# Attention with a per-head bias: ScalarE instead of SyncE issues the loads of the next head group's bias

## The reference

```python
x = x + tanh(g_xattn[0]) * L0_xattn(layernorm(x), ctx, ctx, mask, relative_bias, ...)
# inside, with B, S, H, DH = 4, 512, 16, 16; relative_bias is (1, H, S, S) in float32
scores = einsum('bhqd,bhkd->bhqk', q, k) / sqrt(DH) + relative_bias
attn = softmax(where(mask, scores, -inf), axis=-1)
out = einsum('bhqk,bhkd->bhqd', attn, v)
```

## Time and profile before

| What | Value |
|---|---|
| Time, median of 3 runs | 987.95 us (987.23 to 991.28) |
| The profiled execution's own time | 987.71 us |
| Its span | 986.0 us |
| PE busy | 926.7 us, 94% |
| ACT, POOL, DVE busy | 508.7, 547.7, 581.9 us |
| Attention of the first layer, tiles of L624 | from 63.7 us to about 283 us |

### The profile page before, as it was taken

The page is one execution under the profiler, slowest core; times in us unless marked ns, Lnnn a source line. Parts: engine busy times, 40 slices in busy tenths (PEclk is TensorE's granted clock), DMA queues, the critical chain, the costliest instruction groups (busy, mean ns, idle before and its releaser), DMA issues. The chain is left out here.

```text
span 986.0 us, 22226 instructions
## 1 busy us (share of the span) xinstructions
PE 926.7 (94%) x8245; PEld 541.8 (55%) x8246; DVE 581.9 (59%) x1688; ACT 508.7 (52%) x708; POOL 547.7 (56%) x586
## 2 busy tenths in 40 slices
PE   6989989899989999998999999988899999999998
PEld 2545545454447544454454455456365667777765
DVE  3857878687845634468888888837452222222226
ACT  2428878687863423326888988863301022222221
POOL 4338878688956921127988888851136312222223
PEclk9978999899998999998999999999999999999999
DMA  8572634527104423333242232311922212112217
GB/s 290 195 232 66 205 80 137 151 65 227 46 7 140 150 75 107 96 110 101 66 119 67 86 101 65 89 38 53 331 58 88 75 51 60 64 59 64 64 48 240
DMA packets 99985, 107.63 MB, mean 109 GB/s; under 512 B 18762, under 2 KB 83794, under 8 KB 99890
## 3 DMA queue, kind: packets, MB, share of 16 engines
q1 hardware_dynamic: 89026, 87.79, 29.4%
q10 hardware_dynamic: 7456, 9.18, 2.9%
q0 software_dynamic: 3408, 9.38, 2.7%
HBM read 76.92 MB, written 29.38 MB: 108 GB/s over the span
## 5 line engine op out<-in xcount | busy, mean ns | idle before, releaser
L682 ACT ACTIVATE pT<-ps 128x1024 f32<-128x1024 f32 x256 | 248.3, 1024 | 69.6 <-PE ps L558 69.5
L721 POOL TENSOR_TENSOR s<-nmax,s 128x512 f32<-128x512 f32 x188 | 189.1, 1041 | 37.1 <-DVE nmax L624 37.1
L624 DVE CUSTOM_DVE_ANT_0 xT<-ps,bias 128x512 f32<-128x512 f32 x256 | 166.6, 688 | 44.1 <-PE ps L541 33.5
L721 POOL TENSOR_TENSOR xT<-nmax,xT 128x512 f32<-128x512 f32 x160 | 163.7, 1040 | 38.5 <-DVE nmax L624 38.0
L624 DVE CUSTOM_DVE_ANT_0 s<-ps,bias 128x512 f32<-128x512 f32 x256 | 166.2, 688 | 32.0 <-PE ps L541 21.2
L541 PE MATMUL ps<-ks,qs 48*128 48x512 bf16 (+1 forms) x1024 | 169.3, 393 | 11.7 <-DVE nmax L624 6.6
L573 PE MATMUL ps<-pT,vq 128*32 128x512 f32 x1024 | 135.7, 606 | 5.7 <-ACT pT L682 5.4
L1622 POOL DMA_INDIRECT slots_out<-y,id x39 | 37.7, 968 | 130.6 <-DVE y L1952 123.9
L541 PEld LDWEIGHTS ps<-ks,qs 48*128 48x128 bf16 (+1 forms) x1024 | 39.9, 97 | 126.0 <-DVE nmax L624 93.9
L1706 PE MATMUL ps<-gu,xgT 128*128 x312 | 98.8, 460 | 0.7 <-ACT xgT L1790 0.7
L558 PEld LDWEIGHTS ps<-ident,xT 64*128 64x128 f32 x2048 | 75.0, 139 | 15.5 <-issue 4.6
(11 more groups left out here) (204 smaller groups left out, 1236.8 us busy)
## 6 DMA issues: line engine op xcount, KB each, us to landing
bias<-in_bias SPq DMA_DIRECT2D x14, 1024.0 KB, 7.4
qk_scratch<-parts SPq DMA_DIRECT2D x60, 128.0 KB
qs<-qk_scratch SPq DMA_DIRECT2D x64, 96.0 KB, 2.5
ks<-qk_scratch SPq DMA_DIRECT2D x64, 96.0 KB, 2.4
gu<-in_gate_up SPq DMA_DIRECT2D x8, 704.0 KB, 9.1
slots_in<-zeros SPq DMA_DIRECT2D x4, 1280.0 KB, 6.5
xg<-slots_in SPq DMA_DIRECT2D x39, 130.0 KB
qk_scratch<-parts ACTq DMA_DIRECT2D x36, 128.0 KB
```

Source lines behind the costliest of these rows:

```text
L624: nc.vector.tensor_tensor_reduce(at.s[n % 4][:, k, :], sb.ps[:, ring_bank(tile_place[u]), :], at.bias[:, j if per_head_bias else 0, k, :], ...
L682: nc.scalar.activation(at.pT[:, slot(m // HG, m % HG), 2 * half:2 * half + 2, :], sb.ps[:, 2 + 2 * half:4 + 2 * half, :], ACT.Exp).then_in ...
L721: nc.gpsimd.tensor_tensor(s, at.nmax[:, n % 4, k:k + 1].to_broadcast([P, S]), s, ALU.subtract).then_inc(pool_less_max, 1)
```

## The change

In each of the first three groups, the four bias loads of the next group leave SP's program. ACT issues them instead, in the steps of the last batch (`b == B - 1`): the load of slice `j` stands after the previous step's subtraction (and in step 15 after `keep_out`) and ahead of the exponentials of its own step. It waits for the same semaphore value as before. There are 12 such DMAs in all, of the same size, from the same source to the same place.

```diff
--- before.py
+++ after.py
@@ -516,10 +516,6 @@
                 if not last:
                     sp.wait_ge(scores_done, (hg * 4 + 4) * 16 + 16)
                     load_qk(sp, at, dram, per_head_bias, hg + 1, 0)
-                    for j in range(HG if per_head_bias else 0):
-
-                        sp.wait_ge(biased, at_order[hg * M + M - HG + j, QT - 1] + 1 + 2)
-                        load_bias(sp, at, bias_dram, hg + 1, j)
             groups(sp, body)
 
         @block.tensor
@@ -700,6 +696,9 @@
                         keep_out(*before(hg, b))
                     if first and m == 0:
                         subtract_max(1)
+                    if per_head_bias and b == B - 1 and not last:
+                        act.wait_ge(biased, at_order[hg * M + m, QT - 1] + 1 + 2)
+                        load_bias(act, at, bias_dram, hg + 1, j)
                     exps(hg, m, 0, exp0)
                     exps(hg, m, 1, exp1)
                     if not (last and m + 2 >= M):
```

## The result

The changed kernel is slower: the ratio of its time to the kernel before is **1.0104, 95% interval 1.0068 to 1.0140**, the medians are 996.93 and 987.95 us in nine executions each. Forecast were 1008 us and a range from 998 to 1020. The sign is right. The rise is about 10 us in place of 20.

A forecast was written before the change was run, and what follows sets the result against it. PE, busy 94% of the span, was taken as the bound, with 12.2 us lost at three boundaries. Each would lose 9.3 plus 1.5 us, 32.2 in all: +20.0 on 987.71, hence 1008 us, range 998 to 1020.

The forecast's parts named there:

- The boundaries, and only they: All time lost or gained lies at the three group boundaries, which would lose 32.2 us in place of 12.2.
- j = 0 at nothing: First bias load at a boundary: issued about 1 us later than by SP, landing about when needed, no cost.
- j = 1 issued before 113: Sign in the trace at the first boundary that would prove the forecast wrong; it expected issue at about 115.5.
- j = 1 behind step 12, issued at 115.5 and landing after 7.0 us: First boundary: load issued about 5 us later than now, lands at 122.5, stalling PE more than 4 us at tile 65.
- The chain through `keep_out` to j = 3: First boundary: PE's stall delays keep_out; j = 3 leaves at 127.0, lands at 132.4, and turn_out comes 9.3 us late.
- 1.5 us of lower clock behind the second stall: At each boundary, PE's slower clock after the wait at tile 73 adds 1.5 us, making 10.8.
- SP ... starts the next `load_qk` some 2 us earlier; ... that gives nothing: SP, rid of four issues at a boundary, starts this load sooner; needed only a batch later, it counts as nothing.
- even with 8 us: j = 2, issued near 118.5, lands by 126.5, covered by the wait for j = 3; uncovered, up to 1 us.
- the disputed price: Landing time of j = 1 on ACT's queue beside load_qk: between 5.3 and 10.5 us, taken as 7.0.
- the first rival: Loads on ACT's queue slow beside load_qk, j = 1 taking 10.5 us: 3.5 us more per boundary, 1018 us; chance 0.15.
- The moment of issue as the whole cause: At the boundaries, time from issue to landing stays on the path; the change moves only when loads are issued.
- The rival from the Trainium skill: Issuing from ACT only saves SP's issue time at the boundaries, so slightly faster: fourth rival, 985 us, chance 0.03.

The follow-up runs named there:

- e6_no_loads: The kernel before without the bias loads of groups 1 to 3 and DVE's waits for them; ratio 0.9889.
- e1: The change, but ACT issues j = 0 and 1 together ahead of step 12's exponentials, j = 2 and 3 together ahead of step 14's; ratio 1.0061.
- e7: e1 with SP also holding the next load_qk until DVE is done with the old group's last tile; ratio to the kernel before 1.0076.
- e10: The kernel before with j = 2 and 3 moved to ACT as a pair ahead of step 14's exponentials, SP keeping j = 0 and 1; ratio 1.0095.
- e12_change_no_qk: The change without the load_qk of batch 1 in groups 1 to 3; ratio to the kernel before 1.0057.
- e9: The kernel before with j = 0 and 1 moved to ACT as a pair ahead of step 12's exponentials, SP keeping j = 2 and 3; ratio 0.9987.
- e5_split: The kernel before, SP issuing, with each bias load cut into four 256 KB tiles, each with its own issue, semaphore and DVE wait; ratio 0.9890.
- e11_split_act: The change with each bias load cut into four tiles with a semaphore each, all issued by ACT at the change's places; ratio to the kernel before 1.0089.
- e4_no_ahead: The change, with ACT also waiting for the previous step's second exponential ahead of each bias load; ratio to the kernel before 1.0093.
- e3_j3_early: The change, but j = 3 issued together with j = 2 ahead of step 14's exponentials; ratio to the kernel before 1.0079.
- e2: The change, but j = 1 issued together with j = 0 ahead of step 12's exponentials; ratio to the kernel before 1.0084.

## Why the prediction was half right

- **The boundaries, and only they.** Right: the 9.5 us of added loss there go with the 10.3 of the ratio, and e6_no_loads gives 11 us where the earlier trace rows had 12.2.
- **j = 0 at nothing.** Right. I had it leave about 1 us later than from SP; it left 1 us earlier, since ACT runs ahead. The sign "j = 1 issued before 113" came true on the clock (110.81), but this execution stands 3.3 us ahead; on the scale of the kernel before it is 114.1.
- **j = 1 behind step 12, issued at 115.5 and landing after 7.0 us.** Right as a mechanism, both terms too large. Counted from the matmuls of tiles 64 and 65 (112.40 here, 115.71 before), it left 1.6 us ahead of them in place of 0.2, and landed in 5.6 us. I had named 0.6 us as the most that ACT could run ahead; it was 1.4. Together 2.8 us at the first boundary.
- **The chain through `keep_out` to j = 3.** Right in the trace of the change: `keep_out` idles 3.18 us for PE, and j = 3 goes out with it. I had it leave at the end of `keep_out`, it leaves at the start (0.6 us). With j = 1 too early to stall PE for long, the chain is the shorter; `turn_out` is 6.1 to 6.3 us late in place of 9.3. In addition I gave each boundary 1.5 us of lower clock behind the second stall, and the first boundary had none. These mis-sizings, 10.5 us over the three boundaries (32.2 - 21.7), are the difference between 20 and 10 us.
- **"SP ... starts the next `load_qk` some 2 us earlier; ... that gives nothing", and j = 2 landing "even with 8 us".** This step was wrong, though the change itself shows little of it. I asked only for the deadline of `load_qk` and not for what it takes away. The bandwidth term stood in my text for j = 1, as the disputed price and the first rival; it hardly fell on j = 1 (5.6 us) but on j = 2 (10.3 us), and on j = 3 where that is issued in time (e1, e7, e10: over 11 us). The cover that I gave j = 2 mostly held: in the change tile 72 waited 0, 0.29 and 1.10 us. What `load_qk` costs in the change is the distance to e12_change_no_qk, 4.7 us, and the two intervals overlap.
- **The moment of issue as the whole cause.** Wrong. e1_pairs and e7_pairs_hold give ACT places as good as SP's, and keep 6 and 7.5 us of the loss. e12_change_no_qk, in which no `load_qk` competes, keeps 5.6 us of late places. The two don't add up to a sum; I read it so that whichever makes j = 3 late sets the time. Shown is that the queue of j = 2 and 3 matters by itself, by e9 against e7. That on one queue `load_qk` stays behind the bias loads, and on two it goes beside them, fits most landings, but not j = 1 of e10, which was slowed a little by a `load_qk` behind it on its own queue or by j = 2 on the other. What goes on inside the DMA engines is argued, not shown.
- **The range.** It was luck in part. The time by the ratio lies 0.2 us inside the lower end, the raw median outside it. I had reached down to 998 for an issue 0.6 us earlier, and it was 1.4.
- **The rival from the Trainium skill** (DMA: Bandwidth & Descriptors, "Issuing engines are not separate DMA queues"): its first half, that all DMAs run on the same 16 engines and interleave, agrees with e7, e10 and e12. Its second half, that issuing from several engines only saves the sequencer's time for the issue, does not hold here: which queue j = 2 and 3 stood on was worth 9 us between e7 and e9. The same page, "Queues, rings and completion order", says that each engine takes turns between the queues that have work. By that rule a load of 1 MB beside `load_qk` on another queue is slowed by it; 11.1 to 11.8 us in e7 against 7.9 to 9.3 in e9 agree.

## What to carry to other kernels

Before a load with a near deadline moves to another engine's queue, look at which transfers it stood ahead of: here the move put it beside small, patient loads, and for six loads of 1 MB (j = 2 and 3 at three boundaries) the other queue cost 9 us with hardly anything else changed (e7 against e9). Where a buffer is refilled for the next round, cut the load, its wait and its semaphore to the piece that is used at once: that took away all the stalls (e5_split, 11 us), and no choice of the issuing engine did. The cut alone is not enough: issued by ScalarE at the change's late places it gave nothing (e11_split_act, 1.0089).

## What the runs showed of the hardware

- ScalarE issued DMAs before the instructions ahead of them in its program had run: j = 0 at 105.71, with one exponential of 1.02 us and a subtraction still to come. With a wait on the completion of the previous exponentials it came 1.45 us later (e4_no_ahead). A DMA in ScalarE's program has to be guarded by a semaphore for all that it overwrites, which here it is.
- A load of 1 MB with no other such load in flight and no next `load_qk` beside it took 5.2 to 5.7 us (j = 0 of the change). j = 3, which left while j = 2 was in flight for 2 to 3 us more, took 5.1, 5.5 and 6.6. One that left 0.8 us ahead of `load_qk` took 5.6 at all three boundaries of the change, but 7.6 once in e3_j3_early. One that left 1 us behind the start of `load_qk`, with another load in flight for 1.6 to 1.9 us more, took 8.0 (e1, e2), and one with `load_qk` and 3.8 us of another load beside it 10.3. Without `load_qk` this last took 7.8 (e12).
- PE idled 1.69 + 0.23 us at tile 65 and the clock fell (0.56 in the mean from 117 to 122 us). Behind 1.16 + 0.23 us at 233.12 before, it had not the earlier trace rows. But the length of the stall did not decide it: at the third boundary of the change PE idled 1.70 + 0.23 us, and the clock stayed at 1.00. Stretches of the change as in the earlier trace rows, behind the two stalls:

```profile
117.00:122.00 5.00, 4.55 (x26) 1.30 (x28) 2.97 (x11) 1.22 (x3) 4.04 (x4) 0.56 0.95 288
...
234.00:239.00 5.00, 4.60 (x60) 1.84 (x60) 3.67 (x12) 2.69 (x4) 4.39 (x5) 1.00 1.06 319
```
